# Attention in one pipelined stream, routed experts by sorted rows, and a shifted slot order in the delta phase

## The reference, cut to what matters

```python
# layer 0, attention: 16 heads of 16
attn = einsum('bhqd,bhkd->bhqk', rope(q), rope(k)) * 16 ** -0.5
out = einsum('bhqk,bhkd->bhqd', softmax(attn), v)          # then out @ out_w.T + out_b
# layer 0, experts: 16 of inner size 176, two chosen per token, and a shared one of 352
scores = softmax(einsum('th,eh->te', x, gate_w))
topk_w, topk_idx = top_k(scores, 2)
combine = sum(one_hot(topk_idx, 16) * topk_w[..., None], axis=1)
h = silu(g) * u                                            # g, u: halves of x @ w_gate_up[e]
y = einsum('eti,eih,te->th', h, w_down, combine) + swiglu(x @ shared_gate_up) @ shared_down
# layer 1: a gated delta rule with 32 value heads of 128 in pairs over 16 key heads,
# then a feed-forward with integer weights of inner size 1024
```

## Time and profile before

| | us |
|---|---|
| median of 3 runs (lowest, highest) | 5368.45 (5366.02, 5373.12) |
| the profiled execution's own time | 5360.82 |
| its span | 5359.1 |
| PE busy, share of the span | 4373.6, 82% |
| DVE busy | 3189.1, 60% |
| ACT busy | 2271.8, 42% |
| POOL busy | 1984.2, 37% |

### The profile page before, as it was taken

The page is one execution under the profiler, slowest core; times in us unless marked ns, Lnnn a source line. Parts: engine busy times, 40 slices in busy tenths (PEclk is TensorE's granted clock), DMA queues, the critical chain, the costliest instruction groups (busy, mean ns, idle before and its releaser), DMA issues. The chain is left out here.

```text
span 5359.1 us, 80406 instructions
## 1 busy us (share of the span) xinstructions
PE 4373.6 (82%) x24902; PEld 2742.8 (51%) x24902; DVE 3189.1 (60%) x7272; ACT 2271.8 (42%) x5709; POOL 1984.2 (37%) x4815
## 2 busy tenths in 40 slices
PE   3578888889399994688888888888888888888757
PEld 2312222223266663466666666666666666666534
DVE  4277777770333334577777777767777777777532
ACT  2515555555011111455555555545555555455310
POOL 0000000000000000566666666666666666666400
PEclk7759999998699996899999999999999999999878
DMA  0000000000100000011111111111111111110000
GB/s 24 0 0 0 0 0 0 0 0 2 73 0 0 0 0 14 22 22 30 30 30 22 30 30 30 22 29 30 29 22 30 30 30 22 29 30 18 14 25 16
DMA packets 233239, 98.18 MB, mean 18 GB/s; under 512 B 215922, under 2 KB 220275, under 8 KB 230388
## 3 DMA queue, kind: packets, MB, share of 16 engines
q1 hardware_dynamic: 232948, 94.57, 7.1%
HBM read 75.43 MB, written 18.87 MB: 18 GB/s over the span
## 5 line engine op out<-in xcount | busy, mean ns | idle before, releaser
L1529 POOL TENSOR_TENSOR dl_blocks_tmp<-dl_blocks_l,dl_blocks_x 128x60 f32<-128x60 f32 (+24 forms) x1984 | 715.9, 361 | 426.5 <-DMA dl_blocks_l<-lm_dram 285.8
L509 DVE TENSOR_REDUCE part_max<-mx 128x1 f32<-128x512 f32 x1024 | 639.8, 684 | 218.9 <-PE mx L410 214.1
L1534 POOL TENSOR_TENSOR dl_blocks_x<-dl_blocks_x,dl_blocks_tmp 128x60 f32<-128x60 f32 (+24 forms) x1984 | 708.2, 357 | 155.5
L468 ACT ACTIVATE normed_t<-sc 128x1024 f32<-128x1024 f32 x512 | 497.7, 1021 | 342.5 <-PE sc L403 341.1
L1699 DVE SCALAR_TENSOR_TENSOR dl_conv<-dl_raw,dl_weights,dl_conv 128x512 f32<-128x512 f32 x768 | 578.1, 786 | 23.6 <-ACT dl_conv L1460 15.1
L1249 PE MATMUL prep<-normed_t,dl_weights 128*128 128x512 f32 x1024 | 511.3, 625 | 23.0 <-DMA dl_weights<-in_w_delta 17.2
L410 PE MATMUL mx<-k_t,q_t 96*128 x1024 | 385.4, 413 | 98.6 <-DVE part_max L509 66.7
L1415 ACT ACTIVATE dl_gated_t<-gate_y_ps 128x256 f32<-128x256 f32 x256 | 98.4, 384 | 729.7 <-PE gate_y_ps L1346 729.7
L715 PE MATMUL gu_ps<-w_gate_up,moe_x 128*128 128x352 f32 x1152 | 371.2, 463 | 35.0 <-DMA w_down<-in_wdn 35.0
L381 POOL COPY v_staged<-v 128x16 f32 x256 | 50.6, 198 | 892.7 <-PE o_ps L420 892.0
L1234 PE MATMUL prep<-dl_kq 128*128 128x256 f32 x512 | 179.5, 483 | 243.6 <-DVE dl_v_scaled L1668 243.6
(11 more groups left out here) (234 smaller groups left out, 8939.5 us busy)
## 6 DMA issues: line engine op xcount, KB each, us to landing
dl_blocks_l<-lm_dram SPq DMA_DIRECT2D x256, 128.0 KB, 2.6
dl_weights<-in_w_delta SPq DMA_DIRECT2D x16, 1032.0 KB, 4.9
lm_dram<-dl_lm SPq DMA_DIRECT2D x256, 32.0 KB, 1.6
xs_dram<-dl_blocks_x SPq DMA_DIRECT2D x256, 32.0 KB, 2.0
dl_inverse_t<-xs_dram SPq DMA_DIRECT2D x256, 32.0 KB, 1.9
w_gate_up<-in_wgu SPq DMA_DIRECT2D x6, 1056.0 KB, 10.4
w_down<-in_wdn SPq DMA_DIRECT2D x1, 3200.0 KB, 21.9
residual<-in_x SPq DMA_DIRECT2D x1, 2048.0 KB, 8.5
```

What stands on the lines that cost most here:

```text
L468: act.activation(probs[:, kt % 2, u * 2 * BQ:(u + 1) * 2 * BQ], flat(sc[u][:, :, :]), ACT.Exp, scale=float(DH) ** -0.5).then_inc(s["exp_do ...
L509: dve.reduce_max(part_max[:, qt, b:b + 1], mx[b % 2][:, :], AX.X).then_inc(s["mx_free"], 1)
L1529: pool.tensor_tensor(out, L[:, 0:i, i].unsqueeze(1).broadcast_to([P, NM - c0, i]), Xs[:, c0:NM, i:i + 1].broadcast_to([P, NM - c0, i]), AL ...
L1534: pool.tensor_tensor(Xs[:, c0:NM, 0:i], Xs[:, c0:NM, 0:i], out, ALU.add).then_inc(s["solve_step"], 1)
```

## The change

Three parts change; the phases between them keep their work.

1. **Attention** has no hardware loop any more. All 256 steps (16 heads x 16) are written out; step t makes the maxima of step t and the scores of step t - 20 (`LAG`), without a break between heads. The maxima, the turned maxima ("rows") and the turned output ("out") share a ring of three PSUM banks. One POOL copy per head stages v, in place of 16.
2. **Experts.** The two shared halves stay dense (32 units). For the routed ones the router computes for each token and choice a row number (`slot`): rows sorted by expert, each expert's rows padded to whole tiles of 128, at most 47 tiles. POOL scatters the normed rows to DRAM by 32 indirect DMAs, SP loads tile after tile, PE reads the tile's expert number into a register and runs `turn_x`, `up`, `turn_h`, `down` for that one expert; SP writes the tile's result to DRAM; when all are written, POOL gathers two rows per token by 32 indirect DMAs, and DVE adds them with the two weights.
3. **Delta phase**: other slots and other banks. The turned values go to the merge banks `IB`, so that the key products wait for `exp_done` and no longer for `scale_v`; `lower` stands a slot earlier and `scale_v` after it; POOL takes 25 rows in `FIRST_ROWS` and 6 in `LAST_ROWS`, and `root` ahead of `norm`. SP's stream is the same.

The semaphores of `norm_phase` are now shared by all its calls.

```diff
--- before.py
+++ after.py
@@ attention_phase
+    LAG = NT + 4
+    RING = 3
+    STEPS = HEADS * NT
...
+            for t in range(LAST):
+                e = t - LAG
+                if t < STEPS:
+                    maximum(t, 0)
+                if 0 <= e < STEPS:
+                    scores(e, 0)
+                if t < STEPS:
+                    maximum(t, 1)
+                if 0 <= e < STEPS:
+                    scores(e, 1)
+                if t < STEPS:
+                    maximum(t, 2)
+                if 0 <= e - 1 < STEPS:
+                    weigh(e - 1)
+                if t < STEPS:
+                    maximum(t, 3)
+                for kind, i, _ in fills(t):
+                    if kind == "rows":
+                        turn_rows(i)
+                    if kind == "out":
+                        turn_out(i)
...
@@ moe_phase, SP
+            def rows_in(i):
+                if i >= 4:
+                    sp.wait_ge(s["x_turned"], i - 3)
+                sp.dma_start(xg[i % 4][:, :], a["rows_dram"][i * P:(i + 1) * P, :]).then_inc(x_in[i % 4], 16)
+
+            def rows_out(i):
+                sp.wait_ge(s["y_copied"], NT + i + 1)
+                sp.dma_start(a["back_dram"][i * P:(i + 1) * P, :], yo[i % 4][:, :]).then_inc(y_out[i % 4], 16)
+
+            sp.wait_ge(s["scattered"], 16 * 2 * NT)
+            for i in range(ROUTED_TILES + 3):
+                if i < ROUTED_TILES:
+                    rows_in(i)
+                if i >= 3:
+                    rows_out(i - 3)
...
@@ moe_phase, POOL
+            for t in range(NT):
+                for k in range(2):
+                    pool.indirect_dma_start(a["rows_dram"], bass.IndirectOffsetOnAxis(ap=slot_at[:, k, t:t + 1], axis=0),
+                                            normed[:, t, :], None).then_inc(s["scattered"], 16)
+            pool.wait_ge(s["scattered"], 16 * 2 * NT)
+            for i in range(4):
+                pool.wait_ge(y_out[i], 16 * len(range(i, ROUTED_TILES, 4)))
+            for t in range(NT):
+                for k in range(2):
+                    pool.indirect_dma_start(back[k][:, t, :], None, a["back_dram"],
...
@@ moe_phase, PE
+            for u in range(N_U + 2):
+                if N_S <= u + 1 < N_U:
+                    i = u + 1 - N_S
+                    if i == 0:
+                        pe.wait_ge(s["tiles_ready"], 1)
+                    numbers[i] = pe.value_load(expert_at[0:1, i:i + 1], min_val=0, max_val=EXPERTS - 1)
+                    turn_x(u + 1)
+                if u < N_U:
+                    up(u)
+                if 0 <= u - 1 < N_U:
+                    turn_h(u - 1)
+                if u >= 2:
+                    down(u - 2)
...
@@ delta_heads
-FIRST_ROWS = range(BLK - 1, 10, -1)
-LAST_ROWS = range(10, 0, -1)
+FIRST_ROWS = range(BLK - 1, 6, -1)
+LAST_ROWS = range(6, 0, -1)
...
             def products(p, i):
                 if i == 0:
+                    pe.wait_ge(s["keys_done"], 4 * p + 4)
+                else:
                     pe.wait_ge(s["exp_done"], 2 * p + 1)
-                else:
-                    pe.wait_ge(s["vr_done"], 2 * p + 1)
...
@@ delta_heads, DVE
                         if slot == 4:
                             flush(prep, 1)
-                            scale_v(prep, 0)
+                            lower(prep, 0)
                         if slot == 5:
-                            scale_v(prep, 1)
-                            lower(prep, 0)
-                        if slot == 6:
                             lower(prep, 1)
                             weigh(prep, 0)
+                        if slot == 6:
+                            weigh(prep, 1)
+                            scale_v(prep, 0)
                         if slot == 7:
-                            weigh(prep, 1)
+                            scale_v(prep, 1)
```

More of the change, by code:

```diff
@@ L358, in attention_phase, with fills @@
         block = ctx.enter_context(nc.Block())
[L360 to L367 removed]
+        def fills(t):
+            e = t - LAG
+            out = [("max", t, b) for b in range(QB)] if t < STEPS else []
+            if t % NT == 0 and 1 <= t // NT <= HEADS:
+                out.append(("rows", t // NT - 1, 0))
+            if e % NT == 1 and 1 <= e // NT <= HEADS:
+                out.append(("out", e // NT - 1, 0))
+            return out
@@ new lines, in scores @@
+            def scores(e, u):
+                h, kt = divmod(e, NT)
+                if kt == 0 and u == 0:
+                    pe.wait_ge(s["rows_in"], 16 * MAX_ROWS * (h + 1))
+                if e:
+                    pe.wait_ge(s["exp_done"], 2 * (e - 1) + u + 1)
+                for b in range(2):
+                    last = pe.matmul(sc[u][:, b, :], KT[0:SCORE_ROWS, h, kt * P:(kt + 1) * P],
+                                     QT[0:SCORE_ROWS, h, (2 * u + b) * BQ:(2 * u + b + 1) * BQ], start=True, stop=True)
+                last.then_inc(s["sc_done"], 1)
@@ L1586, in _ @@
                     for i in FIRST_ROWS:
[L1587 removed]
+                        if rec is not None and i == 19:
                             root(QC * rec + 2)
```

845 lines of the change are left out of this document (455 added, 390 removed).

## The result

The changed kernel takes 5007.8 us (median of 4 runs, 5005.6 to 5016.4) against 5367.2 for the kernel before on the same chip: a ratio of 0.9333, 95% interval 0.9317 to 0.9349. The forecast was 4935, with a range of 4780 to 5110. The gain is 359 us where 433 were expected.

A forecast was written before the change was run, and what follows sets the result against it. Bounds: attention's PE-DVE handshake, PE streaming the experts, delta's SP-DMA-POOL ring. 5360.8 - 198 (attention) - 132 (experts) - 104 (delta) = 4927 us profiled; the runs' median lies 7.6 above: 4935 us, range 4780 to 5110.

The forecast's parts named there:

- Attention, -198 forecast: Attention phase: with a third bank PE bounds a step at 2.76 us, 784 us in sum against 982.
- the heads' ends: Attention: DVE's chain and division at a head's end hold up the ring, charged 2.4 us a head, 36 in sum.
- Experts, -132 forecast: Experts' stage: shared units, routed tiles and bare gathers end at 1910 us against 2042.
- the ring that the text names: Routed tiles: PE, ACT's copy, SP's store, SP's load, back to PE bound a tile at 7.8 us, ends 6.5 and 9.7.
- tiles at PE's pace: Rival: routed tiles take 3.1 us, the loads being ahead after all; 202 us less, 4733 us; chance 0.08.
- Indirect DMAs, 1.4 us forecast: Experts' scatters and gathers on POOL: 1.4 us each; 32 scatters hidden behind the shared units, gathers bare at 52 us.
- The rival of 12.8 us for 128 rows: Experts: POOL makes indirect-DMA descriptors one row at a time, 12.8 us a DMA, total 5630 us; chance 0.05.
- Delta, -104 forecast: Delta phase: the period falls from 45.1 to 43.4 us as a wait leaves the ring, 62 x 1.68 us.
- The 1.68 us wait: Delta phase: SP's wait for DVE's `dl_lm`, 1.68 us a period, claimed to leave the ring of SP, DMA and POOL.
- 0 to -110: Delta phase: the ends given for the change in time there, around the forecast of -104 us.
- the period does not shorten: Rival in the delta phase: another wait takes the place of the one removed, total 5040 us; chance 0.17.
- the case I took: Whole kernel, including the delta phase: the likeliest case, delta's period shortened to 43.4 us, 4935 us in total; chance 0.62.

The follow-up runs named there:

- e3: The changed kernel with a ring of two PSUM banks in attention, where it has three: 5108.1 us, ratio 0.9506.
- e2: The changed kernel with SP storing routed tile i-5 behind the load of tile i, where it stored tile i-3: 4791.7 us, ratio 0.8922.
- g9: The changed kernel once more, unchanged, on one chip with g10 and g11: 5006.9 us, ratio 0.9334.
- e5: The changed kernel with DVE's second `lower(prep, 1)`, which completes `dl_lm`, moved to the head of slot 5, before corrections and gate: 5014.7 us, ratio 0.9338.
- g12: The changed kernel with DVE's `dl_conv` multiply-adds on 32 of their 512 columns, instructions and waits the same: 4736.8 us, ratio 0.8819.
- e8: e5 and e2 together, plus `dl_lm` stored before `dl_inverse_t` is loaded and POOL's fourth root before row 10 of the solve: 4751.0 us, ratio 0.8853.
- e1: The changed kernel with the delta phase of the kernel before (slots, banks, rows, roots): 5053.3 us, ratio 0.9405.
- e4: The changed kernel with SP storing `dl_lm` first in a delta period, ahead of the store of the solved blocks: 5267.7 us, ratio 0.9804.
- g11: g10 with the solved blocks turned in slot 7, not 6, and POOL's third root before row 16, not 19: 4645.7 us, ratio 0.8658.
- g10: e5 and e2 together, plus `dl_lm` stored ahead of the load of `dl_inverse_t`, roots as in the changed kernel: 4670.8 us, ratio 0.8698.

## Why the prediction was right, and where it fell short

**Attention, -198 forecast, -194 measured.** The steps went nearly as the text has them: 2.84 us (2.76), the end at 1088 (1085), PE without idle time within them. That the sum fits so well is in part luck. 236 steps at 0.08 us more are 19 us too little in the text, and the heads' ends, priced at 2.4 us, took 1.65 (one step of 3.28 and one of 4.05 in each head), 11 us too much. The mechanism, a third bank that takes DVE's release off PE's path, is shown by e3, at half of the gain; I had not priced bank and order apart.

**Experts, -132 forecast, -125 measured** (from the projection to the first norm of the delta phase; from the router's load to DVE's last addition at 1721.3 it is -128). The shared units were done, and the first rows turned at 1312.5, 114 us after the router's load was issued (1198.3); the text has 1507 - 1391.5 = 115.5. The routed tile was to take 7.8 us and took 7.97, by the ring that the text names: store 0.36 (0.45), load to turn 2.15 (2.6), PE 5.0 (3.8), ACT and handovers 0.45 (0.6) in the tile shown. The sum is nearer than its terms: PE's part, priced for a granted clock of 0.74, ran at 0.66 and was 1.2 us too small; the other three were 0.7 too large, and the text's 0.35 for address instructions has no row. So the path is right and the 2% are luck. e2 shows the ring to be the cause, and the rival "tiles at PE's pace" to be one edit away. Its price there, 3.1 us a tile, was near (2.84). What I left out there is that without the waits the clock rises too, so that taking them away is worth more than they last.

**Indirect DMAs, 1.4 us forecast, 1.27 measured.** The rival of 12.8 us for 128 rows fell: 128 rows of 1 KB take 0.95 us of POOL. Of the reads at 102 cycles each, by the Trainium skill, page GPSIMD Engine Reference, section Performance pitfalls for Q7 kernels, these rows show nothing. By the Trainium skill, page DMA: Bandwidth & Descriptors, section Anatomy of one DMA, a DMA of 128 KB issued by POOL takes 2.3 us. POOL's gathers took 2.8 us from issue to landing and its scatters 3.0 in the median, 0.5 and 0.7 more; SP's load of the same size, which that section is not about, took 2.1 to 2.4. As a price for 32 of them in a row any of these would have been wrong, since POOL sends the next one before the last has landed: the scatters came every 1.29 us all the same.

**Delta, -104 forecast, about -36 measured: the step that failed.** It reads "The 1.68 us wait leaves the ring; the rest of SP's and POOL's pieces stay". Neither half held.

The wait left only two periods of three. Where all is well `dl_lm` is ready 5.4 us after the solve, half a microsecond ahead of SP (5.85); in the other periods it comes at 7.2. The windows of a late period and of one in time show why, and below them PE's rows in these two stretches:

```profile
3208.00:3215.00 7.00, 6.61 (x18) 4.61 (x19) 2.25 (x10) 3.62 (x9) 6.05 (x15) 0.60 0.07 12
3252.00:3259.00 7.00, 5.96 (x31) 4.68 (x31) 4.42 (x18) 5.17 (x18) 5.97 (x16) 1.00 0.03 5
```

```profile
3208.39 0.69 PE L1486 MATMUL gate_y_ps<-ident,dl_gated 128*128 128x128 f32 x2 [3.89 <-DVE dl_gated L1767]
...
3212.72 1.49 PE L1372 MATMUL prep<-dl_kq 128*128 128x256 f32 x4
...
3253.12 0.44 PE L1486 MATMUL gate_y_ps<-ident,dl_gated 128*128 128x128 f32 x2 [1.04 <-DVE dl_gated L1767]
...
3255.34 1.03 PE L1372 MATMUL prep<-dl_kq 128*128 128x256 f32 x4
```

In the late one the granted clock is 0.60 after PE had idled 3.9 us for `dl_gated`, which itself waits for POOL's fourth root inside the solve, and the work up to the key products, which `dl_lm` needs, lasts longer (1.92 us in place of 1.02 for two rows of line 1350, 1.49 in place of 1.03 for the products). The other periods agree. Of 55, the 21 late ones have a granted clock of 0.61 to 0.80 in the 7 us around the end of the solve, and the 34 in time have 1.00. PE had idled 0.2 to 2.7 us for `dl_gated` before the ones in time and 2.2 to 3.9 us before the late ones (up to 3.5 and 2.2 to 4.3 in g9). So the low clock goes with the late `dl_lm` every time, and with a long idle time only mostly; no run took that idle time away alone. I had compared typical times ("ready before SP has issued its load") with a margin of half a microsecond. e5, which brings the late ones to 6.0 us, takes nearly all of these waits away, 4.0 us being left of 24.7, and 20 us of the time between the norms.

And POOL's piece did not stay: the solve grew by 0.54 us. g12 shows that `dl_conv` lengthens POOL's rows. Over 55 periods of each trace it lay beside 18.4 of POOL's rows a period after the change and beside 14.8 before, and all that the rows lasted beyond the shortest of their form is 4.69 us a period after and 4.08 before. These 0.61 us account for the growth; a run that only moves the convolution was not made, so that the new slot order brought them is argued.

The bound "0 to -110" of this term held the result, and the rival "the period does not shorten", at 0.17, was nearer to what happened than the case I took.

The forecasts that rest on a ring I could read row by row (routed tiles, attention step) came within 4%, with the luck said above. The one that rests on the absence of a wait missed by two thirds. Two small slips in the text change nothing: DVE would be free at 1430.0, not 1429.5, and indirect DMAs of 2.6 us would add 45 us, not 47.

## What to carry to other kernels

Count how many steps ahead a load is really issued, along the queue's own order: with a store that waits for the newest result ahead of it, four buffers prefetch nothing. Here three microseconds of waiting in each tile also took PE's granted clock from 1.00 to 0.66, so the wait was worth more than its length. When you take a wait out of a ring, ask by what margin it is gone, and whether the engines that now run side by side slow each other down.

## What was not expected of the hardware

POOL's rows of the solve take about twice as long while DVE runs `dl_conv` (128x512, all operands in SBUF): 0.65 us against 0.33 for one form. It is not any work of DVE: of the 54 rows in 55 periods that had a `dl_gated`, 128x128 from SBUF, and nothing else of DVE beside them, none was long. But it is not `dl_conv` alone either. In the kernel before, 101 of 103 rows beside a `dl_attn` of line 1663 were long, an instruction of another kind, also 128x512 with all operands in SBUF (DVE first, then POOL):

```profile
3635.72 0.43 DVE L1663 TENSOR_SCALAR dl_attn<-dl_attn 128x512 f32<-128x512 f32 x1 [1.08 <-ACT dl_attn L1442]
...
3635.78 0.50 POOL L1529 TENSOR_TENSOR dl_blocks_tmp<-dl_blocks_l,dl_blocks_x 128x35 f32<-128x35 f32 x1
```

Of 54 rows beside an instruction of 64x512 that reads PSUM (`dl_merge`) none was long, nor any beside a `dl_conv` cut to 32 columns in g12. What these have in common, the length, the memory or both, was not varied alone and is open.

An indirect DMA of 128 rows of 1 KB holds POOL for 0.95 us, in either direction, and they follow one another every 1.27 to 1.29 us.

The stage of the shared units took 25 to 32 us longer in e5 to e8 and g12, five kernels on two chips, than in the changed kernel and in e1 to e4 and g9 to g11, the last seven on two other chips. In the trace of e5 ACT stands three times in a row for 8 to 9.5 us. In that stretch PE and DVE stand too, PE once for 12.0 us in which it waits for nothing that the profile shows. The DMAs move 412 GB/s in the 10 us of the first pause and 116 and 106 GB/s in the next two tens; the changed kernel moves 418, 121 and 107 there and has no pause:

```profile
1249.44 0.32 ACT L847 ACTIVATE moe_silu<-moe_gu_ps 128x176 f32<-128x176 f32 x1 [8.23 <-remote]
1259.24 0.38 ACT L837 ACTIVATE branch<-moe_y_ps 128x256 f32<-128x256 f32 x1 [9.48 <-remote]
1269.04 0.32 ACT L847 ACTIVATE moe_silu<-moe_gu_ps 128x176 f32<-128x176 f32 x1 [9.42 <-remote]
```

e8 and g10 differ in one root of a later phase and in these pauses, so the edits are hardly the cause. What the engines waited for is open, and so is whether the chip is the cause: the changed kernel did not run on the two chips with the pauses.
